# Two fused blocks on one core: new orders for all five engines, scores and attend scores in longer runs

## The chip, the cores and the metric

The kernel runs on one core of a Trainium2 chip. Its time is the device time of one execution in microseconds (us); of several runs the median counts. A core has five engines that work in parallel, each through its own list of instructions in order: TensorE (PE, matrix products into PSUM banks), VectorE (DVE), ScalarE (ACT), GpSimd (POOL) and SyncE (SP, which here issues the DMAs). They wait for one another by semaphores.

## The reference

Input are 8 batches of 256 tokens with 128 numbers each, in float32. Two blocks follow each other:

```
xn = layernorm(x)
x  = x + attention(xn; 16 query heads, 4 key heads, width 8) + experts(xn)
       # attention: softmax(q k^T / sqrt(8)) v, then Wo
       # experts: top 2 of 8 gates, but all experts share relu(xn w1) w2
xn = layernorm(x)
x  = x + ssm(xn) + ffn(xn)
       # ssm: xz = xn W_in; causal convolution of 4 taps; silu; dt = softplus(xs W_dt + b)
       #      h_t = h_(t-1) * exp(-A dt_t) + B_t, 16 states; y = sum(h) + D xs; (y silu(z)) W_out
       # ffn: silu(xn w1) * (xn w2), gelu(. h1), gelu(. h2), then w3; 512 wide
```

## The kernel before, in words

The program is written as pieces: a piece is a few instructions of one engine, with the waits that they need. `run_order` goes through a text with the names of the pieces, one text for each engine (`ORDERS`, lines 72 to 125), and issues them in that order, counting how often each name came. So the whole order of the work is that table. What an instruction waits for is written in the piece; nothing is planned at run time.

First block, one batch of 256 tokens after the other, on TensorE:

- `S` (`scores`): the scores of two heads for 128 queries, laid out queries by keys, 16 pieces a batch. VectorE takes the row maximum of each (`M`, line 680). The first 8 are one float32 product (line 388); from piece 8 on each is two bf16 products over 48 rows (line 399). There are three PSUM banks, so score n waits until maximum n-3 is done.
- `A` (`attend_scores`, line 422): the scores again, transposed and with the negated maximum folded in as three more rows, 16 a batch; ScalarE exponentiates each (`E`, line 630), from three other banks. For batches 0 to 6 they use rows 64 to 114 of the array, and the scores rows 0 to 47. For batch 7 they take 115 rows.
- `pv` (line 435): probabilities times values, 4 a batch; `o_out` on ScalarE copies the sum (line 565), `heads` (line 445) transposes it, `back` and `proj_out` bring it through Wo.
- `ffn_in` and `ffn_out` (lines 459, 467) are the experts, `v_gate`, `project` and `project_keys` the projections, `max_rows` (line 489) transposes the maxima, `xn_transposes` the input. `warm` (line 513) are 16 pieces of two products whose result isn't used.
- At the start the keys are copied into four wide tiles on ScalarE (`own_keys`, line 615), each of which two of the first 8 scores need.

Second block, four groups of 512 tokens: `x_transposes`, `x_in`, `wx`, `step_in` on TensorE feed the state space part; `ffn`, `second` (line 1016) and `third` (line 1028) are the feed forward part. For each of 16 states `b` (line 989) spreads one row over the partitions into a bank, ScalarE makes the decays (`D`, line 1217), VectorE runs the recurrence (`scan`, line 1312, two a state), GpSimd adds them up (`add`, line 1368, two a state; four states may be held). `y` (line 1376) multiplies by the gate, `out` (lines 1089, 1099) projects. `b` of state s waits for the scans of state s-2. `b_in` on ScalarE (lines 1175, 1176) and `split` on GpSimd (lines 1381 to 1385) prepare the rows of the next group.

Some pieces share one bank, `half0` or `half1`. The names in `X_AFTER`, `Q_AFTER`, `M_AFTER`, `T_AFTER` and so on (lines 140 to 155) say after which piece the bank is taken over: x is the transposed input, q the query projection, v the values and gates, m the maxima, t the output on its way back, p the projection.

Of the kernel before, what the change touches and what calls it, by code (L numbers as in the profile page):

```python
# [65 lines left out]
def settled(eng, sem, v):  # L66
# [6 lines left out]
    sync="""x_in head x_in constants0 ffn_weights 2*put 2*put_keys x_in put put_keys fetch 2*put_keys 2*put put_keys  # L73
        put fetch put stack 2*rows put rows put fetch stack 3*put 3*rows fetch loads put_keys 3*put put_keys stack put
        2*rows put_keys rows fetch stack 2*put 3*rows stack fetch loads 3*put fetch 3*rows put loads stack rows put
        rows put rows fetch stack 6*rows loads 3*b_rows out b_rows 7*out landed""",
    tensor="""9*warm xn_transposes 2*warm project project_keys ffn_in warm v_gate S xn_transposes S warm ffn_in
        xn_transposes S xn_transposes S project_keys project 6*S ffn_out 2*S xn_transposes 2*S project ffn_in 2*S
        xn_transposes ffn_in max_rows 3*S 2*warm v_gate warm 3*S ffn_out S xn_transposes S 2*A S xn_transposes S A S
        project_keys S A S 2*A S project S A S A ffn_in A S A max_rows A S A S v_gate ffn_in S A S A S ffn_out project  # L80
        A S A S A S pv A S A S pv A S A S A S 2*pv A 2*S project heads A S A S max_rows A S pv v_gate A S A S A S pv
        back A S A S A S pv proj_out pv S 3*A S heads S 2*A S A S back ffn_in proj_out A S A S ffn_in A S A S A S
        max_rows ffn_out v_gate A S A S A S pv A S A S 3*pv S 2*A S A S heads A S A S project ffn_in A S A S back
        ffn_in A S proj_out ffn_out max_rows A S A S A S project ffn_in A S A S A S v_gate ffn_in v_gate A S A S
        ffn_out A S A S A S 2*pv S A S A S 2*pv S 2*A S A S heads max_rows S A S A back ffn_in A S proj_out ffn_in A S
        A S A S ffn_out A S A 2*S 3*pv S A S A S pv A S v_gate heads 2*A S A S back ffn_in proj_out A S A S max_rows
        ffn_in A S 2*A S x_transposes A S A S ffn_out A S A S x_in A S A S pv A S A S pv A S A pv A S A pv A S 2*A S
        heads A ffn 3*A pv 2*A max_rows ffn x_in 2*pv x_in A ffn x_in wx pv A 2*step_in back x_transposes heads ffn b
        A proj_out x_in A x_in b A pv second A second A x_in second A x_in b A wx A step_in b A pv A second b back A
        second A b second A proj_out b A 2*pv 2*b second heads second b step_in third back b third b third proj_out b  # L90
        third b 3*third b third x_transposes b 2*x_in b 2*ffn x_in b x_in ffn wx ffn b 3*out b second 2*out b out
        second b second b second b 2*second b step_in b second b second step_in b third x_transposes b third b x_in b
        2*third x_in third b third b 2*third b ffn x_in ffn b x_in b wx ffn step_in out b ffn out b out b out second
        out b second out b second b 2*second b 2*second b second b step_in b 2*third 2*b 2*third b third b 2*third b
        third b 2*ffn out b ffn b out ffn 2*out 2*b 2*second b second b 2*second b second b second b second 2*out b
        2*third 2*b 6*third 6*out""",
    scalar="""roots deviation0 xn_out deviation0 wide_out q_out k_out own_keys normalised own_keys relu xn_out
# [1402 lines left out]
```

## Time and profile before

| | us |
|---|---|
| median of 3 runs | 357.62 (357.3 to 357.71) |
| the profiled execution | 357.89 |
| its span | 356.1 |
| TensorE busy by the records | 348.4 (98%) |
| VectorE busy | 307.3 (86%) |
| ScalarE busy | 291.1 (82%) |
| GpSimd busy | 232.6 (65%) |

A matmul record's end is modelled and overlaps the next, so the busy time of TensorE hides short waits. The distance from one matmul's start to the next one's start tells more. The profiled execution's own time is 1.8 us above its span.

### The profile page before, as it was taken

The page shows a single profiled execution, that of the slowest core. Times are in us where ns is not written, and L with a number is a line of the kernel's source. Part 1 is how long each engine was busy: PE and PEld are TensorE (multiplying, and loading weights), DVE is VectorE, ACT ScalarE, POOL GpSimd, SP SyncE. Part 2 cuts the span into 40 slices and gives each one's busy share as a digit, 9 for nine tenths or more (in the row PEclk, how much of TensorE's full clock was granted, in tenths as well). Part 3 has the DMA queues.
Part 4 walks back from the last instruction along what each step waited for, and adds up shares of the span by engine and source line. Part 5 has one row for each costly group of instructions (what it writes and reads, how often), then busy time and mean ns, then how long its engine had stood idle before and what let it go on. Part 6 is the DMA issues. An engine that isn't in the chain of part 4 may idle for free.

```text
span 356.1 us, 5750 instructions
## 1 busy us (share of the span) xinstructions
PE 348.4 (98%) x1754; PEld 181.6 (51%) x1754; DVE 307.3 (86%) x530; ACT 291.1 (82%) x508; POOL 232.6 (65%) x294
## 2 busy tenths in 40 slices
PE   7999999999999999999999999999999999999996
PEld 5556544747565523443444447444457444564446
DVE  5898889988899886499999999999999989799940
ACT  3875976877787885898899999999999999899620
POOL 0484457214420601344999989999898999999980
PEclk9999999999999999999999999999999999999999
DMA  4455776586724003000000000000000200000000
GB/s 167 130 146 119 146 204 143 81 131 196 197 78 74 6 0 123 22 1 2 0 0 23 3 0 24 15 0 1 1 2 0 67 0 1 2 0 1 31 0 29
DMA packets 28943, 19.26 MB, mean 54 GB/s; under 512 B 4241, under 2 KB 27889, under 8 KB 28657
## 3 DMA queue, kind: packets, MB, share of 16 engines
q1 hardware_dynamic: 28912, 18.90, 21.8%
q8 instruction: 14, 0.23, 0.3%
q14 instruction: 17, 0.13, 0.1%
HBM read 13.32 MB, written 5.37 MB: 53 GB/s over the span
## 4 chain that ended last, share of the span: by engine, by line
PE 87%; issue 5%; DVE 4%; POOL 2%; ACT 1%; POOLq 0%
PE bank L1028 15%; PE bank L1016 13%; PE bank L435 6%; PE bank L422 5%; PE bank L467 4%; PE bank L399 4%; PE bank L459 4%; PE bank L1005 4%; PE bank L1099 4%; PE bank L1006 4%; PE bank L989 4%; PE bank L1072 3%; PE bank L1052 3%; POOL acc L1368 2%; PE bank L388 2%
## 5 line engine op out<-in xcount | busy, mean ns | idle before, releaser
L1368 POOL TENSOR_TENSOR acc<-acc,hb 128x512 f32<-128x512 f32 x128 | 158.2, 1273 | 19.2 <-DVE hb L1312 18.9
L1312 DVE TENSOR_TENSOR_SCAN hb<-da,bank 128x512 f32<-128x512 f32 x128 | 146.0, 1200 | 9.2 <-PE bank L989 9.1
L680 DVE TENSOR_REDUCE mx<-bank 128x2 f32<-128x512 f32 x128 | 81.7, 682 | 7.2 <-PE bank L399 5.9
L1217 ACT ACTIVATE da<-dt,nega 128x510 f32<-128x510 f32 x128 | 81.4, 710 | 0.3 <-DVE da L1336 0.2
L1016 PE MATMUL bank<-sil,ld 128*128 128x512 f32 x128 | 59.5, 593 | 0.0
L1028 PE MATMUL bank<-gelu,ld 128*128 128x512 f32 x128 | 58.0, 592 | 0.0
L630 ACT ACTIVATE pt<-bank 128x512 f32<-128x512 f32 x72 | 39.6, 602 | 6.2 <-PE bank L422 4.5
L422 PE MATMUL bank<-q_st,k_st 51*128 51x512 bf16 (+1 forms) x128 | 39.8, 382 | 0.4
L1028 PEld LDWEIGHTS bank<-gelu,ld 128*128 128x128 f32 x128 | 24.3, 190 | 26.8 <-issue 25.4
L399 PE MATMUL bank<-k_st,q_st 48*128 48x256 bf16 x240 | 36.9, 272 | 0.0
L1016 PEld LDWEIGHTS bank<-sil,ld 128*128 128x128 f32 x128 | 24.0, 190 | 24.6 <-issue 22.9
L630 ACT ACTIVATE hb<-bank 128x512 f32<-128x512 f32 x56 | 30.4, 600 | 4.4 <-PE bank L422 4.4
L989 PE MATMUL bank<-b_parts,sel 96*128 96x512 bf16 x64 | 23.8, 382 | 0.5 <-DVE hb L1312 0.4
L399 PEld LDWEIGHTS bank<-k_st,q_st 48*128 48x128 bf16 x240 | 17.4, 94 | 10.6 <-DVE mx L680 5.9
L422 PEld LDWEIGHTS bank<-q_st,k_st 51*128 51x128 bf16 (+1 forms) x128 | 9.3, 94 | 22.7 <-ACT pt L630 11.0
L435 PE MATMUL bank<-pt,v_sb 128*32 128x512 f32 x144 | 18.6, 602 | 0.0
L1281 DVE SCALAR_TENSOR_TENSOR xc<-bank,ld,xc 128x510 f32<-128x510 f32 (+2 forms) x24 | 17.7, 742 | 0.7
L1099 PEld LDWEIGHTS bank<-ld,gelu 128*128 128x128 f32 x128 | 16.0, 192 | 3.4 <-issue 3.2
L1052 PE MATMUL bank<-xnT,ld 128*128 128x512 f32 x32 | 16.7, 607 | 0.9 <-ACT xnT L1168 0.9
L459 PE MATMUL bank<-xnT,w 128*128 128x256 f32 x64 | 17.1, 390 | 0.0
L1217 ACT ACT_TABLE_LOAD x13 | 16.7, 1283 | 0.2
L1005 PE MATMUL bank<-xnT,ld 128*128 128x512 f32 x32 | 16.7, 603 | 0.0
(166 smaller groups left out, 527.3 us busy)
## 6 DMA issues: line engine op xcount, KB each, us to landing
q_st<-q_scr SPq DMA_DIRECT2D x15, 192.0 KB, 3.8
q_st<-q_scr SPq DMA_DIRECT2D x7, 384.0 KB, 5.3
ld<-in_pack SPq DMA_DIRECT2D x2, 1024.0 KB, 5.5
q_scr<-qk_parts SPq DMA_DIRECT2D x8, 192.0 KB, 2.5
k_st<-k_scr SPq DMA_DIRECT2D x14, 96.0 KB, 4.5
q_scr<-qk_parts SPq DMA_DIRECT2D x8, 128.0 KB, 2.7
out<-x SPq DMA_DIRECT2D x8, 128.0 KB, 2.0
ld<-in_pack SPq DMA_DIRECT2D x1, 968.0 KB, 7.6
```

Of the source, the lines that this page charges most:

```text
L399: last = mm(score_bank(b, n)[:, j * T:(j + 1) * T], q_st[b % 2][0:ROWS, 2 * pair + j, q * P:(q + 1) * P], k_st[b % 2][0:ROWS, 2 * pair // ...
L422: mm(st(b, n)[:, :], k_st[b % 2][lo:, kv, kt * P:(kt + 1) * P], q_st[b % 2][lo:, h0:h0 + 2, :].rearrange("r h n -> r (h n)"), start=True, ...
L435: last = mm(bP[kv * VW:(kv + 1) * VW, :], v_sb[b % NV][:, kt, kv, at:at + VW], prob(b, 4 * grp + kv), start=(grp == 0), stop=(grp == 3))
L459: last = mm(bP[:, j * T:(j + 1) * T], w1[:, c * P:(c + 1) * P], xnT[b], start=True, stop=True)
L630: act(prob(b, n), st(b, n)[:, :], ACT.Exp, scale=HD ** -0.5).then_inc(p_ok, 1)
L680: eng.tensor_reduce(mx[:, 2 * pair:2 * pair + 2, q], score_bank(b, n)[:, :].rearrange("p (h k) -> p h k", h=2), AX.X, ALU.max).then_inc(mx ...
L989: mm(b_bank(g, s)[:, :], sel[:, s, :], b_parts[:, g % 2, :], start=True, stop=True).then_inc(b_ps, 1)
L1016: last = mm(f_bank(g, c)[:, :], h1[:, k, c * P:(c + 1) * P], sil[:, k, :], start=(k == 0), stop=(k == KC - 1))
L1028: last = mm(f_bank(g, c)[:, :], h2[:, k, c * P:(c + 1) * P], g2[:, k, :], start=(k == 0), stop=(k == KC - 1))
L1217: act(da(n)[:, :, 1:T], dt[:, g % 2, c, :].rearrange("p (b n) -> p b n", b=GB)[:, :, 1:T], ACT.Exp, scale=nega[:, c, s:s + 1]).then_inc(da ...
L1312: eng.tensor_tensor_scan(hb[:, s % NPAIR, c, :], da(n).rearrange("p b n -> p (b n)"), b_bank(g, s)[:, :], 0.0, ALU.mult, ALU.add).then_inc ...
L1368: TT(acc[:, g % 2, c, :], acc[:, g % 2, c, :], hb[:, s % NPAIR, c, :], ALU.add).then_inc(add_ok, 1)
```

## The change

All five texts of `ORDERS` are replaced by others with the same pieces, each as often as before. No piece is changed. Since pieces stand in another order, three of the tables that name after whom a shared bank is taken over are changed as well. The diff (the table cut to one line of each kind):

```diff
 ORDERS = dict(
-        2*warm xn_transposes 2*warm project project_keys ffn_in warm v_gate S xn_transposes S warm ffn_in
...
-        A S A S A S pv A S A S pv A S A S A S 2*pv A 2*S project heads A S A S max_rows A S pv v_gate A S A S A S pv
+        A S A S A S 2*pv A S A S A S pv A S A S A S pv A S max_rows heads A S A S A S v_gate pv A S A S A S back pv
...
-Q_AFTER = "x0 x3 x4 k2 v2 q4 v4 m4"
+Q_AFTER = "x0 x3 x4 k2 v2 p0 v4 m4"
...
-M_AFTER = "x5 q3 q5 p1 p2 v6 p4 m6"
-T_AFTER = "v3 p0 q6 m5 v7 m7 p5 p6"
+M_AFTER = "x5 q3 q4 p1 p2 v6 p4 m6"
+T_AFTER = "v3 q5 q6 m5 v7 m7 p5 p6"
```

**TensorE, batch 1, around `heads` of batch 0.** L422 is an attend score, L399 x2 a score, L445 `heads`, L489 `max_rows`, L435 `pv`. Before:

```order
L520 MATMUL bank<-xnT,head 128x256
L445 MATMUL bank<-head,o_sb 128x128 x4
L422 MATMUL bank<-q_st,k_st 128x512
L399 MATMUL bank<-k_st,q_st 128x256 x2
L422 MATMUL bank<-q_st,k_st 128x512
L399 MATMUL bank<-k_st,q_st 128x256 x2
L489 MATMUL bank<-head,mx 32x128
L422 MATMUL bank<-q_st,k_st 128x512
L399 MATMUL bank<-k_st,q_st 128x256 x2
L435 MATMUL bank<-pt,v_sb 32x512 x4
```

Now:

```order
L422 MATMUL bank<-q_st,k_st 128x512
L399 MATMUL bank<-k_st,q_st 128x256 x2
L489 MATMUL bank<-head,mx 32x128
L445 MATMUL bank<-head,o_sb 128x128 x4
L422 MATMUL bank<-q_st,k_st 128x512
L399 MATMUL bank<-k_st,q_st 128x256 x2
L422 MATMUL bank<-q_st,k_st 128x512
L399 MATMUL bank<-k_st,q_st 128x256 x2
L422 MATMUL bank<-q_st,k_st 128x512
L399 MATMUL bank<-k_st,q_st 128x256 x2
L497 MATMUL bank<-cst,xnT 128x40 x2
```

After `heads` stood a run of two pairs and a run of one, with `max_rows` between; now there is one run of three pairs, and `max_rows` stands before `heads`. Only one pair and `max_rows` are left between the last `pv` of batch 0 and `heads`; before these were an attend score, two scores and a `project`.

**ScalarE, the start.** L615 x2 is a piece of `own_keys`, L559 x2 a normalised batch, L569 a copy of transposed input, L582 a `relu`. Before:

```order
L604 ACTIVATE qk_parts<-bank,cst 32x256
L615 ACTIVATE hb<-dt,cst 128x256 x2
L559 ACTIVATE xn<-x_sb,nmr,rstd 128x128 x2
L615 ACTIVATE hb<-dt,cst 128x256 x2
L582 ACTIVATE hT<-bank 128x512
L569 ACTIVATE xnT<-bank 128x256
L559 ACTIVATE xn<-x_sb,nmr,rstd 128x128 x4
L569 ACTIVATE xnT<-bank 128x256 x2
```

Now:

```order
L604 ACTIVATE qk_parts<-bank,cst 32x256
L559 ACTIVATE xn<-x_sb,nmr,rstd 128x128 x2
L615 ACTIVATE hb<-dt,cst 128x256 x2
L559 ACTIVATE xn<-x_sb,nmr,rstd 128x128 x2
L569 ACTIVATE xnT<-bank 128x256
L559 ACTIVATE xn<-x_sb,nmr,rstd 128x128 x2
L569 ACTIVATE xnT<-bank 128x256
L582 ACTIVATE hT<-bank 128x512
L569 ACTIVATE xnT<-bank 128x256
```

The first `own_keys` comes behind a normalised batch, and the fourth (not in these rows) behind the query and key copies of the next group, right ahead of the first exponential of the gates.

**TensorE, the end.** L989 is a `b`, L1028 x2 a `third`, L1016 x2 a `second`, L1089 and L1099 are `out`. Before:

```order
L1099 MATMUL bank<-ld,gelu 128x128 x4
L989 MATMUL bank<-b_parts,sel 128x512
L1028 MATMUL bank<-gelu,ld 128x512 x4
L989 MATMUL bank<-b_parts,sel 128x512 x2
L1028 MATMUL bank<-gelu,ld 128x512 x12
L1089 MATMUL bank<-wout_half,y 128x128 x8
```

Now:

```order
L989 MATMUL bank<-b_parts,sel 128x512
L1028 MATMUL bank<-gelu,ld 128x512 x4
L989 MATMUL bank<-b_parts,sel 128x512
L1028 MATMUL bank<-gelu,ld 128x512 x4
L989 MATMUL bank<-b_parts,sel 128x512
L1028 MATMUL bank<-gelu,ld 128x512 x8
L1089 MATMUL bank<-wout_half,y 128x128 x8
```

The last `b` stood ahead of six pieces of `third`, now ahead of four.

## Rows read from the trace of the kernel before

**Rows 1.** The page: the chain of work that ended last, by engine.

```profile
PE 87%; issue 5%; DVE 4%; POOL 2%; ACT 1%; POOLq 0%
```

**Rows 2.** Busy time by stretch: us, then PE, PEld, DVE, ACT, POOL, PEclk, DMA share.

```profile
45.00:97.00 52.00, 51.68 (x432) 28.51 (x432) 45.79 (x109) 39.15 (x91) 21.47 (x56) 1.00 0.71 162
...
150.00:180.00 30.00, 29.07 (x122) 11.83 (x122) 27.79 (x39) 27.21 (x49) 17.94 (x15) 1.00 0.00 1
180.00:348.00 168.00, 167.44 (x568) 84.80 (x567) 153.16 (x166) 151.09 (x214) 159.59 (x139) 1.00 0.03 9
```

**Rows 3.** The chain in order of time: start, us, what.

```profile
12.70 0.86 PE bank L459 x4
...
66.63 1.06 PE bank L459 x4
...
217.89 0.22 PE bank L989
218.11 1.72 PE bank L1016 x4
...
261.62 0.57 PE bank L1061 x16
```

**Rows 4.** Timeline of PE: start, us, instruction; three pairs, then the maxima.

```profile
67.62 0.39 PE L422 MATMUL bank<-q_st,k_st 51*128 51x512 bf16 x1
...
67.85 0.38 PE L422 MATMUL bank<-q_st,k_st 51*128 51x512 bf16 x1
...
68.38 0.28 PE L489 MATMUL bank<-head,mx 128*32 128x128 f32 x1
```

**Rows 5.** Timeline of PE and of ACT around the first `heads`.

```profile
49.95 1.92 PE L435 MATMUL bank<-hb,v_sb 128*32 128x512 f32 x16
...
51.81 0.61 PE L399 MATMUL bank<-k_st,q_st 48*128 48x256 bf16 x4
52.35 0.70 PE L520 MATMUL bank<-xnT,head 128*128 128x256 f32 x2
...
51.94 0.60 ACT L565 ACTIVATE o_sb<-bank 128x512 f32<-128x512 f32 x1 [0.77 <-PE bank L435]
```

**Rows 6.** Timeline of ACT and PE, the start.

```profile
9.27 0.89 ACT L615 ACTIVATE hb<-dt,cst 128x256 f32<-128x256 f32 x2
...
10.30 1.10 PE L388 MATMUL bank<-hb,dt 128*128 128x512 f32 x2
...
20.43 0.61 PE L399 MATMUL bank<-k_st,q_st 48*128 48x256 bf16 x4
```

**Rows 7.** Timeline of PE and ACT, the rows of group 1.

```profile
164.16 0.65 PE L1061 MATMUL bank<-xs,wx_p 128*32 128x128 f32 x16
164.92 0.39 PE L422 MATMUL bank<-q_st,k_st 115*128 115x512 bf16 x1
165.37 1.98 PE L1072 MATMUL bank<-xs,ld 128*128 128x512 f32 x4
...
165.05 0.27 ACT L1176 ACTIVATE b_full<-bank 128x128 f32<-128x128 f32 x1
```

**Rows 8.** Timeline of PE, DVE and POOL, the end.

```profile
337.43 4.55 DVE L1312 TENSOR_TENSOR_SCAN hb<-da,bank 128x512 f32<-128x512 f32 x4 [0.71 <-PE bank L989]
...
347.74 1.95 PE L1089 MATMUL bank<-wout_half,y 128*128 128x128 f32 x16
...
343.61 2.49 POOL L1376 TENSOR_TENSOR y<-acc,zs 128x512 f32<-128x512 f32 x2
```

**Rows 9.** Timeline of DVE: row maxima behind two runs of three pairs.

```profile
56.70 1.89 DVE L680 TENSOR_REDUCE mx<-bank 128x2 f32<-128x512 f32 x3
```

**Rows 10.** Timeline of PE: those two runs, first row of each.

```profile
56.24 0.39 PE L422 MATMUL bank<-q_st,k_st 51*128 51x512 bf16 x1
...
58.37 0.39 PE L422 MATMUL bank<-q_st,k_st 51*128 51x512 bf16 x1
```

**Rows 11.** The waits: engine, line, waited for, us in total, times, longest.

```profile
DVE mx L680 <- PE bank L399: 5.9, 12, 1.5
```

More of the change, by code:

```diff
@@ L72 @@
 ORDERS = dict(
[L73 to L80, printed above, removed]
-        A S A S A S pv A S A S pv A S A S A S 2*pv A 2*S project heads A S A S max_rows A S pv v_gate A S A S A S pv
[L82 to L96, printed above, removed]
@@ L121 @@
-    gpsimd="""biased G ones split_k split_q 3*G shifted0 4*G biased split_q maxima_split 8*G split_q maxima_split 8*G
-        split_q split_k maxima_split G biased G split_q 5*G maxima_split 5*G split_q 4*G maxima_split 10*G split_q 3*G
-        maxima_split 7*G maxima_split 4*G constants maxima_split split 2*start 8*add start 6*add start 7*add split
-        4*add shifted 7*add 2*y 2*start add split 30*add y add y 3*add 2*start 9*add split 23*add 2*y 29*add 2*y""",
+    sync="""x_in head x_in constants0 ffn_weights x_in put 3*put_keys 2*put fetch put 3*put_keys 2*put fetch put stack
+        put 2*rows put rows stack fetch put 2*rows put rows put put_keys loads fetch 2*put stack put loads 3*rows
+        2*put_keys fetch stack rows put rows 2*put rows fetch 3*put stack loads 3*rows put fetch stack 3*rows put
+        loads put fetch stack 6*rows 3*b_rows 4*out b_rows 4*out landed""",
@@ new lines @@
+    scalar="""roots deviation0 xn_out deviation0 wide_out q_out k_out normalised own_keys normalised xn_out normalised
+        xn_out relu xn_out own_keys k_out own_keys q_out deviation0 own_keys gate_exp relu 2*normalised xn_out q_out
+        normalised relu xn_out normalised negated_maxima relu gate_exp xn_out E xn_out E k_out 3*E q_out 4*E
+        negated_maxima relu 3*E gate_exp relu 3*E q_out 8*E o_out 2*E negated_maxima 4*E gate_exp 3*E o_out 3*E q_out
+        2*E relu 3*E relu negated_maxima 5*E gate_exp 3*E o_out 2*E q_out 2*E relu 3*E relu E negated_maxima 2*E q_out
+        E relu 2*E gate_exp relu 3*E gate_exp 6*E o_out 2*E negated_maxima 2*E relu E relu 3*E deviation 5*E o_out 3*E
+        gate_exp 2*E relu 3*E negated_maxima relu E x_out 2*E decay_rates 5*E taps 3*E o_out 4*E negated_maxima E sil
+        2*E gate_x 3*E sil taps gate_z E gate_x b_in E gate_z o_out E sil 2*dt sil E x_out 2*D E taps 2*D E 2*D taps
+        gate_x D gate_z E 3*D gate_x D E D E D E D gate_z D b_in E 2*D E D E 2*D E D E D E D 2*gelu o_out 2*gelu 2*dt
+        12*D deviation hid normalise hid x_out 2*hid 2*taps sil gate_x sil gate_x 2*gate_z normalise 2*sil b_in 29*D
+        4*gelu dt x_out dt D taps 5*D taps 3*D 4*hid sil gate_x gate_z gate_x sil gate_z 3*D 2*sil b_in 17*D gelu dt D
+        3*gelu dt 13*D 4*hid 2*sil 3*D 2*sil 12*D 2*gelu 3*D 2*gelu 3*D 4*hid""",
@@ L125 @@
+    gpsimd="""G biased ones split_k split_q 2*G shifted0 5*G split_q maxima_split 8*G biased split_k split_q
+        maxima_split 8*G biased split_q maxima_split 5*G split_q 3*G maxima_split 5*G split_q 3*G maxima_split split_q
+        12*G maxima_split 7*G maxima_split 5*G constants maxima_split split 2*start 7*add split 5*add start 5*add
+        start 9*add shifted 5*add y add y 2*start 2*add split 31*add 2*y 3*add start 4*add split 10*add start 18*add y
+        add y 27*add 2*y""",
 )
```

52 lines of the change are left out of this document (29 added, 23 removed).

## The prediction, made before the changed kernel ran

> **What bounds the kernel now.** I read the page first: the chain that ended last is TensorE for 87%, and no other engine has more than 4% of it [rows 1]. Then the busy time by stretch. From 45 to 97 us TensorE is busy for 51.68 of 52 us, VectorE for 45.79 and ScalarE for 39.15; from 180 to 348 us TensorE for 167.44 of 168, GpSimd for 159.59 [rows 2]. As the busy time of TensorE hides waits, I looked at the starts. In the chain a feed forward half takes 1.72 us for 4 records, again and again, with a `b` of 0.22 between [rows 3], and in a run of three pairs the first two attend scores start at 67.62 and 67.85: 0.22 us from pair to pair, whatever VectorE and ScalarE do [rows 4]. So TensorE works like a conveyor, from some 16 us to the last `out`, with short waits at a handful of places. As it has the same pieces before and after, the time changes by two things alone: what it costs TensorE to go from one kind of piece to another, and its waits.
>
> **What a border costs.** Four records of `ffn_in` take 0.86 us where a full-size product stands on either side, and 1.06 where a run of scores does [rows 3]: 0.20 for two borders, so about 0.1 for each. A run of three pairs shows the same: three steps of 0.22 are 0.66, and from its first row to the `max_rows` behind it are 0.76 [rows 4]. Between a score run and `pv` or `max_rows`, and between those and full-size products, the starts show the same 0.09 to 0.10. A border here is a change among three shapes: products over part of the rows (bf16 scores and attend scores of batches 0 to 6), products into 32 columns (`pv`, `max_rows`, `project_keys`, `wx`), and full ones. Between two full ones none is seen: `b`, over 96 rows, costs 0.22 and the `second` behind it 1.72 for its four records [rows 3].
>
> **What a step costs.** An attend score lies beside a score: both together take 0.22 us [rows 4]. One alone takes the same 0.22: a run of one attend score and two scores goes from 51.81 to 52.35, that is two steps and a border, 0.54 [rows 5].
>
> **The change, part by part.**
>
> *Score runs, TensorE.* I counted in both orders. There are 57 runs of partial-row products before and 53 after; 10 of them were three full pairs, now 18. The changes of shape go from 144 to 136. Eight borders less, at 0.095: -0.76 us. The steps of all runs together go from 137 to 135, since fewer scores and attend scores stand without a partner: two steps less at 0.218, -0.44. Together -1.2 us, directly on the conveyor.
>
> *The start.* ScalarE now normalises a batch ahead of the first `own_keys`. That batch takes 0.8 us (as long as a piece of `own_keys`, 9.27 to 10.16), so the first wide keys are done at 10.9 instead of 10.16, and the first score, at 10.30 before, can start at 10.9 [rows 6]. The `xn_transposes` in front of it takes 0.22 of that. Further on `ffn_in` 1 meets a later `relu`, some 0.4, and the fourth `own_keys` ends about 0.8 later. Against that the key copies come 1 us earlier. Walking these through with the rows' durations, the first bf16 score starts at about 20.85 instead of 20.43 [rows 6]; 0.22 of this is a `warm` that stood behind it. I take +0.2. The ends: -0.3, if the earlier third normalisation group (its shift comes sooner from GpSimd) shortens a wait, and +0.8, the whole of the later keys.
>
> *`heads`.* The last `pv` of batch 0 ends at 51.87 (49.95 and 1.92), the copy `o_sb` runs from 51.94 to 52.54, and `heads` needs it, so it could not start before 52.6. Before, the run of 0.54 and a `project` of 0.53, from 51.81 on, cover that [rows 5]. Now one pair (0.22), a border and `max_rows` (0.12) are there and end at 52.25: TensorE waits about 0.4. For batches 1 and 3 runs of 0.76 and some 0.7 stand there; the cover falls short by 0.1 each. Sum +0.6; the ends are 0, if ScalarE's copy comes out of its queue at once and something else was late anyway, and +1.2, twice my value.
>
> *`wx` and `step_in` of group 1.* `step_in` stood one attend score behind `wx`, and waited for the copy of `wx` on ScalarE, 165.05 to 165.32; it started at 165.37 where 165.14 would do, and the `wx` before it took 0.76 to the next start, where that of group 3 takes 0.57 [rows 7]. Now a `second`, a `b` and two attend scores (2.4 us) lie between. -0.4. On ScalarE that copy comes about 4 us of work later; `step_in` comes 4.8 later too, so that it doesn't matter. GpSimd has its `split` of group 1 far earlier, after 7 adds rather than 21, and may wait there for the copy. Between 150 and 180 us it is busy for 17.94 of 30 us [rows 2], so there is room.
>
> *The end.* The last `b` stands 4 records x 4 = 16 records ahead of `out` in place of 24. At 0.43 each it would start at 347.74 - 6.9 - 0.2 = 340.7. Its two scans, 2.3 us, and the last add and the two `y` behind (1.2 and 2.5) end at about 347.2. `out` starts at 347.74, so it is still covered, but with 0.5 us in place of 1.6 [rows 8]. 0, at most +0.5.
>
> *The rest.* Other moves in the second block (sync's order, table loads of ScalarE: 38 before and 37 after, decays up to 8 us of ScalarE's work later) lie beside the conveyor. ScalarE works 151.09 of 168 us there [rows 2], and each late decay that I followed still comes ahead of its scan. 0; if one is late by 1 us, one scan waits for it, which costs nothing as long as `b` and the adds have a state in hand.
>
> Sum: -1.2 + 0.2 + 0.6 - 0.4 = -0.8 us. The profiled execution took 357.89 us, which is 0.27 above the median 357.62; against the median the forecast is 356.8 us. Its own range, by the ends above and by what the waits that exist can do, is 355.6 to 357.6.
>
> **Rivals.**
>
> *The banks hold the longer runs back (slower).* A score waits for the maximum three before it. VectorE takes 1.89 us for three of them [rows 9], TensorE makes three in 0.66. Of two runs of three that start 2.13 us apart, the third score of the second, two pairs behind its start, came at 58.8, and the maximum that it needs ended at 58.59 [rows 9, 10]: 0.23 to spare. A run, one `pv` and a run, as the new order has in batch 1 and later, start 0.76 + 0.96 = 1.72 apart: 0.18 too early. This decides if VectorE can't win back in the gaps: it is busy for 45.79 of 52 us already [rows 2]. For the eight additional runs of three at 0.4 each it is 3.2, so the time is 357.6 - 0.8 + 3.2 = 360.0; at 0.25 each it is 358.8, which I take as its value. Against it: in the old order eight of the ten runs of three take 0.76, without a wait, as in [rows 4]; the other two 0.78 and 0.82. The Trainium skill says in TensorEngine Tiling (Array Packing), section PSUM Bottleneck, that tiling speeds up TensorE but not the emptying of PSUM, which may become the bottleneck; that is this rival. The trace agrees with it only at places: by it alone a pair could not go faster than a maximum, 0.63, and three pairs go in 0.66.
>
> *VectorE takes back what TensorE gains (no change).* VectorE is busy for 88% of the attention stretch [rows 2]. If its list runs through at some place without a gap, what comes before may be 1 us earlier and what comes behind isn't: 357.6. For it: VectorE's work is the same to the last piece. Against it: in the whole kernel its maxima waited 5.9 us for scores [rows 11].
>
> *Old waits go too (faster still).* With the rates above, TensorE's pieces and borders add up to 347 us. Of the span of 356.1, some 4.5 us lie ahead of the first product and behind the last; 4 to 5 us are waits. A new order may have half: 357.6 - 0.8 - 2.2 = 354.6.
>
> *The last states come too late (no change).* If the end above misses by 1 us: 357.6.
>
> **How the numbers follow.** Forecast case 0.45 (356.8), banks 0.22 (358.8), VectorE takes back 0.15 (357.6), old waits go 0.13 (354.6), late end 0.05 (357.6). A measurement of this kernel can tell 0.2%, 0.7 us, from no change. Of the forecast case 0.6 lies below 356.9, the rest within; the bank case lies above 358.3 for nine parts in ten. So faster is 0.27 + 0.13 and a little of the others, which I round to 0.45; slower is 0.20 plus 0.05 of the late end and the start's upper end, 0.25; the same 0.30. The range takes in old waits and banks at their values: 354.4 to 359.2.
>
> **What would show it.** Right: runs of three pairs at 0.76, 53 runs, the chain still TensorE, the first `heads` about 0.45 late, `out` of the last group starting right behind the last `third`. Wrong: runs of three at 0.9 or more, with weight loads of L399 waiting for L680, would be the banks; if the runs are clean and `step_in` of group 1 (before at 165.37 [rows 7]) comes no earlier than its place in the order asks, 4.8 us later, at 170.2, VectorE took it back. A first bf16 score after 21.3 us would mean that the start was underrated.

## The result, and the profile after

| | before | after |
|---|---|---|
| median, us | 357.78 (357.3 to 358.02, 10 runs) | 360.12 (359.11 to 364.17, 10 runs) |
| ratio | | 1.0081, 95% interval 1.0062 to 1.01 |
| the profiled execution | 357.89 | 364.17 |
| its span | 356.1 | 362.4 |

The kernel got 0.8% slower; 356.8 was forecast, and the range ended at 359.2. Eight of the ten runs lie between 359.11 and 360.32; the profiled one is 4 us above the median and another (362.61) 2.5. Over the whole time the granted TensorE clock was 0.991 in the profiled one and 0.995 in the other, and 0.999 or 1.00 in the eight. So two things have to be explained: an ordinary loss, and one that some executions have.

The chain of waits by engine of the kernel after reads as before, with VectorE at 7% for 4 [rows 1]:

```profile
PE 88%; DVE 7%; issue 2%; ACT 2%; POOL 0%; DVEq 0%; ACTq 0%; POOLq 0%
```

Busy time by stretch of the kernel after (us, then PE, PEld, DVE, ACT, POOL, PEclk, DMA share and GB/s), to be held against [rows 2]: in the attention stretch TensorE is busy for 49.23 of 52 us where it was 51.68, and in the last row it is as busy as before (167.71 us for 167.44).

```profile
45.00:97.00 52.00, 49.23 (x402) 28.71 (x405) 44.43 (x109) 35.70 (x79) 20.32 (x57) 0.98 0.74 164
150.00:180.00 30.00, 28.73 (x116) 11.99 (x115) 25.03 (x34) 27.92 (x49) 15.05 (x17) 1.00 0.04 11
180.00:348.00 168.00, 167.71 (x582) 84.05 (x582) 158.06 (x175) 154.20 (x221) 161.13 (x138) 1.00 0.03 8
```

**The long wait of the profiled execution.** Timeline of TensorE, batch 4:

```profile
91.97 0.54 PE L497 MATMUL bank<-cst,xnT 128*128 128x40 f32 x4
94.86 0.58 PE L422 MATMUL bank<-q_st,k_st 51*128 51x512 bf16 x1 [2.35 <-issue]
...
95.24 0.63 PE L422 MATMUL bank<-q_st,k_st 51*128 51x512 bf16 x1
...
96.25 3.64 PE L435 MATMUL bank<-pt,v_sb 128*32 128x512 f32 x16
```

The first attend score of batch 4 waits 2.35 us, and behind it pairs come every 0.4 us instead of 0.22 [rows 4], and 16 `pv` records take 3.64 us. By stretch:

```profile
85.00:90.00 5.00, 5.00 (x37) 3.27 (x35) 3.72 (x12) 3.81 (x10) 3.10 (x8) 1.00 1.06 272
90.00:95.00 5.00, 2.65 (x25) 2.47 (x24) 2.97 (x11) 1.71 (x5) 1.87 (x10) 0.94 1.20 170
95.00:100.00 5.00, 5.00 (x29) 1.61 (x29) 1.89 (x3) 1.57 (x3) 0.00 (x0) 0.50 0.16 33
100.00:105.00 5.00, 4.94 (x40) 1.52 (x33) 2.76 (x5) 3.15 (x7) 0.00 (x0) 0.87 0.00 0
```

The granted clock falls to 0.50, the lower of the two levels (1.2 GHz), near the end of the wait, stays there over the next slice and is 0.87 in the one after. The slices from 90 to 105 us lack 0.06, 0.50 and 0.13 of full clock, each times 5 us: some 3.4 us beside the wait itself (an estimate). What the attend score waits for are three rows of 8 KB that SyncE copies into its tile. SyncE's timeline (start and length of the issue):

```profile
83.22 0.45 SPq L358 DMA_DIRECT2D ld<-in_pack  x1
84.22 2.39 SPq L340 DMA_DIRECT2D q_st<-m_parts  x3
```

The new order puts `loads` 2, weights of the second block, ahead of `rows` 12 to 14. The issues with their size and the time to landing (of three: the median), from the same trace:

```profile
ld<-in_pack SPq DMA_DIRECT2D x1, 1024.0 KB, 10.6
...
q_st<-m_parts SPq DMA_DIRECT2D x3, 8.0 KB, 6.0
```

The last of the three was issued at 85.75 and landed at 94.77, 0.09 us ahead of the attend score. Before, the load was issued at 89.72, behind the rows, and these took a median of 1.9 us (3.8 for the first).

**What the prediction had named.** TensorE of the kernel after: a run of three pairs [rows 4], `heads` of batch 0 [rows 5], the start [rows 6], `wx` and `step_in` of group 1 [rows 7], the end [rows 8].

```profile
68.39 0.39 PE L422 MATMUL bank<-q_st,k_st 51*128 51x512 bf16 x1
...
69.15 0.28 PE L489 MATMUL bank<-head,mx 128*32 128x128 f32 x1
...
53.85 0.28 PE L489 MATMUL bank<-head,mx 128*32 128x128 f32 x1
54.25 0.63 PE L445 MATMUL bank<-head,o_sb 128*128 128x128 f32 x4
...
21.01 0.61 PE L399 MATMUL bank<-k_st,q_st 48*128 48x256 bf16 x4
...
174.22 0.64 PE L1061 MATMUL bank<-xs,wx_p 128*32 128x128 f32 x16 [0.57 <-issue]
...
177.46 1.88 PE L1072 MATMUL bank<-xs,ld 128*128 128x512 f32 x4
...
354.05 1.95 PE L1089 MATMUL bank<-wout_half,y 128*128 128x128 f32 x16
```

This run of three pairs takes 0.76, as before; the others follow with the experiments. `heads` comes 0.40 behind `max_rows`, 0.28 more than its 0.12. The last `y` on GpSimd, below, ends at 353.61, 0.44 ahead of `out`:

```profile
351.12 2.49 POOL L1376 TENSOR_TENSOR y<-acc,zs 128x512 f32<-128x512 f32 x2
```

### The profile page after: what moved, and what is told of

The parts are those of the page before. It is cut to its first block, busy times and chain, and to the rows that moved or that the text cites. A ratio compares the mean times of both kernels' runs of the same rounds, so it can differ in the third digit from the quotient of the medians.

```text
span 362.4 us, 5749 instructions
## 1 busy us (share of the span) xinstructions
PE 350.8 (97%) x1754; PEld 180.9 (50%) x1754; DVE 308.8 (85%) x530; ACT 289.7 (80%) x507; POOL 233.2 (64%) x294
## 4 chain that ended last, share of the span: by engine, by line
PE 88%; DVE 7%; issue 2%; ACT 2%; POOL 0%; DVEq 0%; ACTq 0%; POOLq 0%
PE bank L1028 15%; PE bank L1016 14%; PE bank L435 8%; PE bank L422 5%; DVE mx L680 4%; PE bank L1052 4%; PE bank L1099 4%; PE bank L989 4%; PE bank L1005 4%; PE bank L1072 4%; PE bank L1006 4%; PE bank L467 4%; PE bank L459 3%; PE bank L399 3%; PE bank L1089 2%
## 5 line engine op out<-in xcount | busy, mean ns | idle before, releaser
L680 DVE TENSOR_REDUCE mx<-bank 128x2 f32<-128x512 f32 x128 | 81.7, 681 | 13.4 <-PE bank L399 11.2
L1016 PE MATMUL bank<-sil,ld 128*128 128x512 f32 x128 | 58.9, 592 | 0.0
L1028 PE MATMUL bank<-gelu,ld 128*128 128x512 f32 x128 | 58.4, 592 | 0.0
L422 PE MATMUL bank<-q_st,k_st 51*128 51x512 bf16 (+1 forms) x128 | 39.5, 387 | 2.4 <-issue 2.4
L1028 PEld LDWEIGHTS bank<-gelu,ld 128*128 128x128 f32 x128 | 24.1, 190 | 26.6 <-issue 26.1
L399 PE MATMUL bank<-k_st,q_st 48*128 48x256 bf16 x240 | 37.2, 275 | 0.2 <-DVE mx L680 0.2
L1016 PEld LDWEIGHTS bank<-sil,ld 128*128 128x128 f32 x128 | 23.8, 190 | 23.9 <-issue 23.3
L989 PE MATMUL bank<-b_parts,sel 96*128 96x512 bf16 x64 | 24.1, 382 | 0.5 <-DVE hb L1312 0.3
L422 PEld LDWEIGHTS bank<-q_st,k_st 51*128 51x128 bf16 (+1 forms) x128 | 9.3, 94 | 29.6 <-ACT pt L630 12.1
L399 PEld LDWEIGHTS bank<-k_st,q_st 48*128 48x128 bf16 x240 | 17.5, 95 | 7.9 <-DVE mx L680 3.6
L845 POOL TENSOR_TENSOR m_parts<-negm,m_parts 32x128 bf16<-32x128 f32 x8 | 3.3, 418 | 26.1 <-ACT negm L576 26.0
L435 PE MATMUL bank<-pt,v_sb 128*32 128x512 f32 x144 | 19.9, 652 | 0.0
L1205 ACT ACTIVATE gelu<-bank,ld 128x512 f32<-128x512 f32 x14 | 9.1, 686 | 11.8 <-PE bank L1028 11.7
L1099 PEld LDWEIGHTS bank<-ld,gelu 128*128 128x128 f32 x128 | 16.4, 192 | 3.0 <-issue 2.6
L822 POOL TENSOR_TENSOR gd<-srt 128x16 f32<-128x16 f32 x8 | 1.7, 214 | 24.4 <-issue 13.9
```

The source lines that it names most:

```text
L399: last = mm(score_bank(b, n)[:, j * T:(j + 1) * T], q_st[b % 2][0:ROWS, 2 * pair + j, q * P:(q + 1) * P], k_st[b % 2][0:ROWS, 2 * pair // ...
L422: mm(st(b, n)[:, :], k_st[b % 2][lo:, kv, kt * P:(kt + 1) * P], q_st[b % 2][lo:, h0:h0 + 2, :].rearrange("r h n -> r (h n)"), start=True, ...
L435: last = mm(bP[kv * VW:(kv + 1) * VW, :], v_sb[b % NV][:, kt, kv, at:at + VW], prob(b, 4 * grp + kv), start=(grp == 0), stop=(grp == 3))
L680: eng.tensor_reduce(mx[:, 2 * pair:2 * pair + 2, q], score_bank(b, n)[:, :].rearrange("p (h k) -> p h k", h=2), AX.X, ALU.max).then_inc(mx ...
L989: mm(b_bank(g, s)[:, :], sel[:, s, :], b_parts[:, g % 2, :], start=True, stop=True).then_inc(b_ps, 1)
L1016: last = mm(f_bank(g, c)[:, :], h1[:, k, c * P:(c + 1) * P], sil[:, k, :], start=(k == 0), stop=(k == KC - 1))
```

## The experiments

Each was timed in five rounds, beside runs of the kernel before on the same chip. "Trace" is the profiled span less before's 356.1, both rounded to 0.1.

| kernel | us, median | ratio to before, 95% interval | trace |
|---|---|---|---|
| e1, after again | 359.10 (358.55 to 361.09) | 1.0042, 1.0026 to 1.0058 | +0.7 |
| e2, load 2 later | 359.11 | 1.0034, 1.0022 to 1.0046 | +1.2 |
| e3, all loads later | 359.11 | 1.0033, 1.002 to 1.0045 | +1.2 |
| e4, before, load 2 early | 364.06 | 1.0177, 1.0156 to 1.0198 | +5.3 |
| e5, old start | 358.52 | 1.0023, 1.001 to 1.0035 | +0.9 |
| e6, old to batch 2 | 361.37 | 1.0101, 1.0077 to 1.0125 | +4.3 |
| e7, old first block | 359.04 | 1.0041, 1.0029 to 1.0053 | +1.1 |
| e8, before, 18 borders more | 361.29 | 1.0104, 1.0092 to 1.0117 | +3.4 |
| e9, old to 51 us | 357.87 | 1.0004, 0.9996 to 1.0013 | 0.0 |
| e10, new from 51 to 130 us | 360.96 | 1.0102, 1.0085 to 1.0119 | +2.4 |
| e11, e10, taps later | 360.51 | 1.0086, 1.0073 to 1.0098 | +2.9 |
| e12, before, one batch first | 358.39 | 1.0024, 1.0014 to 1.0034 | +0.7 |
| e13, e11, seam complete | 357.55 | 0.9994, 0.9985 to 1.0003 | -0.4 |
| e14, e3, own keys first | 358.74 | 1.0035, 1.0022 to 1.0047 | +0.8 |

**e1 to e4: the load ahead of the rows.** e1 is the kernel after, unchanged. e2 moves load 2 behind the rows:

```diff
-    ... 2*put rows fetch 3*put stack loads 3*rows put fetch stack 3*rows put loads ...
+    ... 2*put rows fetch 3*put stack 3*rows put loads fetch stack 3*rows put loads ...
```

e3 moves all four loads so (0 behind fetch 3, 1 behind fetch 5, 2 as in e2, 3 behind the last rows). e4 does the opposite to the kernel before:

```diff
-    ... 3*put fetch 3*rows put loads stack rows put ...
+    ... 3*put fetch loads 3*rows put stack rows put ...
```

> The changed kernel once more, to see the profile of another execution: the profiled one took 4 us more than the median of its kind, with a wait of 2.35 us ahead of the first attend score of batch 4 and the granted clock at 0.5 from 95 to 100 us. Theory DMA (the weight load `loads` 2 is queued ahead of the rows of maxima `rows` 12 to 14, whose last part landed at 94.77): the same wait is there, 1 to 3 us long, the third part of the maxima lands 5 us or more after its issue, the median is again 360.1, and an execution of about 360 has less or nothing of the clock's dip. Rival banks (longer runs wait for the maxima and the exponentials): no wait for a DMA at batch 4 in an ordinary execution; 2.3 us more than before are spread over the runs of three pairs, which take 0.8 to 0.9 instead of 0.76.

> The changed kernel with one DMA moved on SyncE's list: `loads` 2 (1 MB of weights) stands behind `put` 21, so behind `rows` 12 to 14, in place of ahead of them. Theory DMA: the rows of batch 4 land within 2 to 3 us, the first attend score of batch 4 waits for nothing, the clock stays at 1.0, and the time falls by 2 to 3.5 us, to 356.8 to 358. Rival banks: no change within 0.5 us, 360.1.

> The changed kernel with all four weight loads at the places that they had on SyncE's list before the change (behind `fetch` 3, `fetch` 5, `put` 21 and `rows` 23). Theory DMA: at or below the kernel with `loads` 2 alone moved, by 0 to 1 us, as the others stand ahead of the maxima of batch 2 and of the query parts of batch 7 too. Rival banks: 360.1, no change.

> The kernel before the change with `loads` 2 moved ahead of `rows` 12 to 14 and behind `fetch` 6, all else as it was. Theory DMA: slower than before by 1 to 3 us, with a wait of the first attend score of batch 4 for the maxima. Rival (the load's place doesn't matter, the runs do): within 0.5 us of 357.7.

e1 had its median at 359.10, not at the expected 360.1. That is the same kernel as in the result, 1.6 us above the kernel before where it was 2.3; where the rest of the 2.3 comes from is open, since there is no trace of an ordinary execution of that series. e2 and e3 have the median of e1, and not the 357 to 358 that the theory gave them; only the upper end moved, from 361.09 to 359.41 and 359.18. In e1's profile the three rows took a median of 5.6 us to land and the attend score didn't wait. So moving the load takes nothing off the 1.6 us. That it costs the new order some executions is argued: the result's profile shows it for one, and the other slow one of that series has the lower clock too; e1's 361.09 has it not (1.00), so something else made it, and twelve executions of e2 and e3 are few. In the old order the same move costs 6.5 us in the median (364.06 against 357.54) and 5.7 at least, where 1 to 3 were expected. e4's chain in order of time, and its stretches:

```profile
91.61 3.62 issue
95.23 0.37 PE bank L423
```

```profile
90.00:95.00 5.00, 1.61 (x15) 1.42 (x13) 2.01 (x6) 2.40 (x11) 0.78 (x4) 1.00 0.79 202
95.00:100.00 5.00, 4.77 (x31) 1.69 (x32) 2.18 (x7) 1.68 (x4) 1.07 (x4) 0.66 0.03 8
```

The same wait, 3.62 us (the old order has `v_gate` elsewhere, so there is less in front of the attend score), and the same fall of the clock behind it. Of the four executions two had a mean clock of 0.995 (363.24 and 363.42 us) and two 0.991 (364.69 and 365.04).

**e5, e12, e14: the start.** e5 is e3 with the old orders of all engines up to the first attend score. e12 is the kernel before with one move on ScalarE, e14 is e3 with that move taken back:

```diff
 e12, ScalarE
-    ... q_out k_out own_keys normalised own_keys relu ...
+    ... q_out k_out normalised 2*own_keys relu ...
 e14, ScalarE
-    ... q_out k_out normalised own_keys normalised xn_out ...
+    ... q_out k_out own_keys 2*normalised xn_out ...
```

> The changed kernel with its four loads behind the rows (as in e3), and with the old orders of all five engines up to the first attend score (24 scores on TensorE, up to the first exponential on ScalarE). Theory: the start was underrated. In the trace of e3 the first bf16 score comes 1.03 us later than before, and nothing behind gives that back, so this kernel is 1.0 us below e3's 359.1: 358.1. Rival: the late start is taken up by a wait behind it (VectorE's list, the next normalised group), and the time stays at 359.1.

> The kernel before, with one move on ScalarE alone: the first normalised batch (0.77 us) stands ahead of the first own_keys, as in the new order. Theory (the start term): the first wide keys and the first scores come about 0.7 us later, and 0.3 to 0.7 of it reaches the end: 358.1. Rival (TensorE has other work there, as the prediction had it, or a later wait takes it up): 357.6.

> The changed kernel with its loads behind the rows (e3) and one move back on ScalarE: the first own_keys ahead of the first normalised batch. Theory (e12 backwards): 0.6 to 0.8 us off e3's 359.1, so 358.4. Rival (what e5 showed: a late start is partly taken up by later waits, here 24 to 51 us): 358.8. Rival (TensorE's own order there has other work between): 359.1.

e12 cost 0.9 us (358.39 against 357.46 beside it). Its TensorE:

```profile
10.97 1.10 PE L389 MATMUL bank<-hb,dt 128*128 128x512 f32 x2 [0.67 <-ACT hb L616]
...
21.10 0.61 PE L400 MATMUL bank<-k_st,q_st 48*128 48x256 bf16 x4
```

(Its lines are one further: L389 is L388.) The first score waits 0.67 us for the keys, the first bf16 score comes 0.67 late [rows 6], and at the end of the trace 0.77 are left: in the old order there is no cover.

In the new order it is another matter. TensorE of e3 and, behind the dots, of e14, ahead of the first score:

```profile
11.39 0.41 PE L506 MATMUL bank<-head,xn 128*128 128x128 f32 x2 [0.66 <-DVE srt L711]
...
11.00 0.41 PE L506 MATMUL bank<-head,xn 128*128 128x128 f32 x2 [0.66 <-ACT xn L559]
```

The new order has `xn_transposes` of batch 1 ahead of the first score and right behind `v_gate`, and by `X_AFTER` it may write only when VectorE has read what `v_gate` left (`v_out`, line 711). That ends at 11.24 in e3 and 10.86 in e14, 0.15 and 0.14 ahead of the transposes, so TensorE waits 0.66 in both, whatever the order of the keys (in e14 the normalised batch that it also needs ends at about the same moment, and the profile names that). In e3 the first keys are done at 11.25, and the first score, right behind the transposes, starts at 11.64. The two kernels are then the same: counted from the first `project`, the first bf16 score comes after 14.16 us in both, and the end after 350.0 in both, as in e1. What differs is the head ahead of the first `project`, 6.91 us in e14 and 7.30 in e3. So e14 gave nothing that its move could claim: its ratio to before is 1.0035 where e3 has 1.0033, and the 0.37 us between their medians, taken on two chips, don't show in the ratios.

e5 has 0.59 less than e3 in the medians, but its trace doesn't gain either: the first bf16 score is back at 20.32, 13.45 behind the first `project`, and by attend score 16 it is 1.06 behind the kernel before again; the end comes 350.1 behind the first `project`. Its head is shorter (6.87). The five traces with the new order's ten `warm` ahead of the first `xn_transposes` start it at 5.82 to 6.10, the eleven with nine at 5.53 to 5.67; that may be where e5's 0.59 lies, but no run changes this alone. So the theory of these three holds in the old order, and the rival ("a late start is taken up by later waits") in the new one.

**e6, e9, e10, e11, e13: which stretch.** These kernels follow the old orders on all five engines up to some moment and the new ones behind it, or old, new, old; loads behind the rows in all. As an example the texts of TensorE at e9's cut:

```diff
 kernel before:
     ... A S A S A S pv | A 2*S project heads A S A S max_rows ...
 e9, the new order behind the cut:
     ... A S A S A S pv | A S A S pv A S max_rows heads A S A S A S ...
```

> As e5, but the old orders reach to score 64 and attend score 41 (the first two and a half batches). Theory: the new attention order gains in borders there what it loses in waits, e3 lies +1.1 to +1.4 us behind at attend scores 32 and 48, so 357.8, some 0.3 below e5. Rival (the new attention order is itself faster and only the start is bad): 358.5 or more, since this takes its gain away.

> The changed kernel with its loads behind the rows, and the old orders of all engines up to the same moment, some 51 us (TensorE up to pv 2, ScalarE up to the first o_out, VectorE up to maximum 44, the row and key transfers that are issued by then). Theory: of e3's distance to before 1.3 us arises ahead of 51 us (TensorE comes to pv 3 1.29 us late, with an order that asks for 0.15 less), and what lies behind gains and loses about the same: 359.1 - 1.3 = 357.8. Rival (as in e5, the waits come back behind the cut, because the new order wants its pieces at other times): 358.5. Rival (the wait of e6 came from any seam between two orders, not from transfers that were out of step with ScalarE): 360 or more, with a slow TensorE behind a long wait.

> As e9, and from attend score 106 on (some 130 us) the old orders again: only the attention between 51 and 130 us is new. Theory: there the new order has 1.1 us less of borders and steps and costs some 0.6 of waits, so it gains 0.4 on before: 357.5 - 0.4 = 357.1, and less than e9. Rival (the borders are hidden or not worth their price there): 357.5 or more. Rival (the seam at 130 us doesn't fit and costs a wait as in e7): 358.5.

e9 fits the theory: 357.87 for 357.8. In the balance all the ordinary loss is made in the first 51 us. e6, expected at 357.8, lost 3.5 us more than e9, since its cut was not at the same moment on all engines: ScalarE kept the old order up to its 40th exponential (some 71 us), SyncE only for 39 pieces (some 45 us). ScalarE and TensorE of e6:

```profile
54.40 0.47 ACT L593 ACTIVATE qk<-bank,cst 128x256 f32<-128x256 f32 x1 [2.17 <-DMA q_scr<-qk_parts]
```

```profile
55.38 0.27 PE L489 MATMUL bank<-head,mx 128*32 128x128 f32 x1 [2.16 <-ACT qk_parts L594]
...
57.17 1.08 PE L497 MATMUL bank<-cst,xnT 128*128 128x40 f32 x4
```

```profile
48.00:56.00 8.00, 5.84 (x55) 2.54 (x54) 4.84 (x11) 5.03 (x11) 3.30 (x6) 1.00 0.60 162
56.00:64.00 8.00, 8.00 (x48) 3.09 (x48) 5.17 (x12) 3.94 (x11) 6.29 (x13) 0.57 0.36 97
64.00:72.00 8.00, 7.85 (x62) 4.18 (x56) 7.27 (x17) 5.32 (x11) 0.53 (x4) 1.00 0.52 72
```

A transfer out of step stops ScalarE for 2.17 us, that stops TensorE for 2.16, and the clock is 0.57 for the eight us behind it. The trace is 4.3 us longer than before's. Three of the six executions had a lower mean clock (0.990 to 0.995) and took 362.2 to 362.8; the other three (1.00) took 359.8 to 360.5. So the clock makes some 2 us of it.

e10, e11 and e13 were to isolate the new attention between 51 and 130 us. e10 and e11, expected at 357.1 and 357.2, failed at the second cut, each time by a wait that belongs to neither order:

```diff
 e10, VectorE (old text behind maximum 124)
     ... M | other_taps 3*M heads clear_keys x_mul ffn_mul ...
 e11, VectorE
+    ... M | 3*M heads other_taps clear_keys x_mul ffn_mul ...
 e13, VectorE and ScalarE
+    ... M | 3*M heads other_taps ffn_mul x_mul clear_keys ...
-    ... E | gate_x E sil 4*E negated_maxima ...
+    ... E | E sil 3*E gate_x E negated_maxima ...
```

> As e10, with the other taps of the first convolution (2.3 us on VectorE) behind the last maxima and heads 5, where the new order has them; in e10 they stood ahead of three maxima and two scores waited 2.2 us. Theory: e10's loss is that seam alone, so this is 3.4 us below e10, 357.2: old up to 51 us, new up to 130 us, old again, with the gain of the new middle, 0.3 to 0.4 on before. Rival (the new middle gains nothing): 357.6 or more.

> As e11, with the rest of the seam mended: on ScalarE the first gate_x, which needs the convolution, behind four more exponentials, and on VectorE the feed forward product ahead of it. In e11 that gate_x waited 2.74 us for VectorE, the exponentials stood behind it, and TensorE came 1.7 and 1.1 us late. Theory: without those waits this is 2.9 + 0.3 below e11's 360.5: 357.2, the new middle's gain. Rival (there is always a next wait at this seam, as conv and the products come 2 to 3 us later than in the old order): 358.0 or more. Rival (the new middle gains nothing): 357.5.

TensorE of e10 (a score waits for VectorE, which runs 2.3 us of taps), and ScalarE of e11 (`gate_x` waits for the taps, the exponentials stand behind it):

```profile
131.66 0.39 PE L399 MATMUL bank<-k_st,q_st 48*128 48x256 bf16 x2 [1.99 <-DVE mx L680]
```

```profile
133.03 0.63 ACT L1152 ACTIVATE xs<-xc 128x512 f32<-128x512 f32 x1 [2.74 <-DVE xc L1281]
```

e10's profiled execution is the only one of its six with the clock at 1.00; the others had 0.995 or 0.991. Of e11's five, four had 0.995, and the one at 1.00 took 359.83. With both waits gone e13 is 3.0 us below e11, with the clock at 1.00 or 0.999 in all executions. At 357.55 beside 357.61 it can't be told from the kernel before; its trace is 0.36 shorter than before's. It is the best of these versions, and not shown to beat the kernel before.

The starts of the profiled executions say where a difference arises. The kernels have the same set of pieces ahead of these places of TensorE's list (the first row is the first `project`, a landmark only):

| TensorE has done | before | e1 | e3 | e9 | e13 | borders fewer in the new order |
|---|---|---|---|---|---|---|
| the head, up to `project` 0 | 6.95 | 6.76 | 7.30 | 6.95 | 6.96 | |
| all ahead of the first bf16 score | 20.43 | 20.92 | 21.46 | 20.52 | 20.40 | 0 |
| its first 64 pieces | 34.48 | 34.30 | 34.84 | 34.32 | 34.22 | 2 |
| its first 117 pieces | 50.83 | 51.58 | 52.12 | 50.79 | 50.70 | 3 |
| its first 349 | 129.52 | 129.85 | 130.39 | 129.18 | 129.10 | 8 |
| its first 422 | 183.65 | 184.42 | 184.97 | 183.75 | 183.28 | 8 |
| all (span) | 356.06 | 356.75 | 357.31 | 356.08 | 355.70 | 8 |

e1 and e3 differ by 0.5 us from the head on: so much does the head of one execution differ from another's, and behind it the two are the same. e3's execution took 359.1, the median, so I go by it. Of its 1.25 us the head has 0.35. At the first bf16 score another 0.68 are lost, but after 64 pieces nothing of that is left (27.54 us behind `project` 0, where before had 27.53): the late start is taken up. Between pieces 64 and 117, from 34 to 51 us, 0.93 are lost again, in e1 as in e3. From 117 to 349 e3 gained 0.42, where five borders less ask for 0.48 and the steps for something more: the rest went into new waits. From 349 to 422, the passage to the second block, it lost 0.45. Behind that the distance stays.

The largest wait between pieces 64 and 117 is that of `project` 3, which by the new `Q_AFTER`, as by the old, may write only behind ScalarE's copy of the keys (line 604). Before and, behind the dots, e3:

```profile
37.24 0.67 PE L520 MATMUL bank<-xnT,head 128*128 128x256 f32 x2 [0.23 <-ACT qk_parts L604]
...
37.73 0.67 PE L520 MATMUL bank<-xnT,head 128*128 128x256 f32 x2 [0.51 <-ACT qk_parts L604]
```

In both it starts 1.76 to 1.77 us behind `project_keys` (35.48 and 35.96), but six pieces stood between them before and three now. In e5 the wait is 0.58, and `project` 3 starts 30.4 us behind `project` 0 in both e3 and e5: here the gain of an early start is gone. Smaller ones follow in e3, 0.15 of `max_rows` for the maxima and 0.25 of `ffn_out` for a `relu`. No run takes them away by themselves.

**The longer runs.** Of the 18 runs of three full pairs in e1 and e3, eleven take 0.76 to 0.80 us to the start of the piece behind, seven 0.82 to 1.08. In three of the seven the third score waits for a maximum; of these the longest, from 51.90 to 52.83 in e3, shows it in the weight loads:

```profile
52.51 0.11 PEld L399 LDWEIGHTS bank<-k_st,q_st 48*128 48x128 bf16 x2 [0.27 <-DVE mx L680]
```

The three take 0.93, 0.89 and 0.88, together 0.42 above 0.76. So the banks do hold some longer runs back, by little. The three longest, 1.04, 1.04 and 1.08, are waits of the `back` and the `ffn_out` behind the run.

**e7: the second block alone.** Old orders up to the last attend score, new ones behind.

On TensorE at the cut:

```diff
-    ... 2*pv b | b second heads second b step_in third back ...
+    ... 2*pv b | b 2*second heads b step_in back third ...
```

> The old orders up to the last attend score; only the second block (from the eighth b on) is in the new order, the loads behind the rows. Theory: all of the difference arises in the first block and at its seam; e3's second block runs at a constant distance to before, so 357.5 to 357.6, no change to before (357.54 measured beside it). Rival (the second block's fewer waits are worth something and only the first block hides it): 357.0 or less. Rival (the new end costs, as its last b stands late): 358.0.

It came out 1.5 us above the theory. Up to its cut the trace is 0.4 ahead of before; then, on VectorE and on TensorE:

```profile
183.20 0.36 DVE L685 RECIPROCAL rden<-bank 128x32 f32<-128x32 f32 x1 [1.49 <-PE bank L445]
```

```profile
188.60 0.39 PE L989 MATMUL bank<-b_parts,sel 96*128 96x512 bf16 x1 [1.34 <-DVE hb L1312]
```

VectorE's old list has the work on `heads` 7 one scan early for the new TensorE list, which does a `second` more ahead of it; VectorE waits, its scans come late, and `b` waits for them. Again the seam, not the block: e7 says nothing on the new second block, and e3's constant distance says that it is worth next to nothing either way.

**e8: the price of a border.** The kernel before, with an attend score and a score moved between two full pieces at nine places:

```diff
-    ... ffn_in S A S A S ffn_out project A S A S A S pv ...
+    ... ffn_in S A S A S ffn_out A S project A S A S pv ...
```

> The kernel before, with one attend score and score moved between two full pieces at nine places of the attention stretch: 18 changes of shape more, same pieces, same count of steps. By the price of the prediction (0.095 us each) 18 cost 1.7 us, so 357.5 + 1.7 = 359.2. Rival: the price is seen only where nothing else waits, and the pairs now stand further apart, which gives VectorE room: 358.2 or less. Rival: the gap in the starts isn't caused by the change of shape at all: 357.5.

It cost 3.7 us (361.29 against 357.58), twice the forecast. TensorE at the place of the diff (`ffn_out`, the moved pair, `project`, two pairs, `pv`; the lines are one further than before's):

```profile
43.65 2.05 PE L468 MATMUL bank<-w,hT 128*128 128x128 f32 x16
45.64 0.39 PE L423 MATMUL bank<-q_st,k_st 51*128 51x512 bf16 x1
...
45.96 0.70 PE L521 MATMUL bank<-xnT,head 128*128 128x256 f32 x2
46.59 0.39 PE L423 MATMUL bank<-q_st,k_st 51*128 51x512 bf16 x1
...
47.13 1.07 PE L436 MATMUL bank<-pt,v_sb 128*32 128x512 f32 x8
```

In the kernel before these pieces start at 43.46 (`ffn_out`), 45.35 (`project`), 45.88 (three pairs) and 46.63 (`pv`). `ffn_out` takes 1.99 to the next start where it took 1.89: 0.10. The moved pair takes 0.32, 0.22 and 0.10. `project` takes 0.63 where it took 0.53: 0.10. The two pairs take 0.54 for 0.75, one step less. Together 3.48 for 3.17, so 0.31 for two more borders. A run between full pieces thus costs 0.3 beside its steps: 0.1 on the piece ahead, 0.1 on its own last start, and 0.1 on the piece behind. That is 0.15 a border, and nine such places make 2.7 us. At eight of the nine the piece behind the moved pair is 0.39 to 0.43 later, as here (0.42). At the ninth, ahead of `ffn_in` 8, it is 0.83, a wait on top. The rest, some 0.5, I haven't placed. The rivals with a border at less, or at nothing, are out.

## Why the prediction was wrong

The sum was -0.8; measured were +2.3 us in the result and +1.6 beside e1. Two steps failed: that new waits were priced at a few places only (the start, `heads`, `wx`, the end), and that SyncE's order was set to nothing.

*What bounds the kernel, the borders and the steps (-1.2).* The conveyor is right: in e9 and e13 the new attention passes from piece 117 to 349 faster than the old one. Two things are wrong. The price of a border was 0.15, not 0.095: the rows were right, but I counted the 0.20 that `ffn_in` shows and the 0.1 at the end of a run [rows 3, 4] as two readings of one price, where they add up to 0.3 for two borders. With it eight borders would be -1.2, and the sum -1.6. The steps are good to 0.2 us only: paired off neighbour by neighbour they are 133 and 132, one fewer, and not 137 and 135. And only 0.4 arrives from piece 117 to 349, where five borders ask for 0.48, by the new price 0.75; the rest went into waits, 0.42 of it into those of the longer runs for maxima.

*The waits that had no term.* This is the first step that failed, and most of the ordinary loss. Between pieces 64 and 117, in the attention of batch 0, the sum had nothing but a border's gain, and e1 and e3 lose 0.93 us there. The largest wait is `project` 3 behind `project_keys`, the case that the prediction had worked out for `heads`: the new order leaves fewer pieces between two that depend on each other through ScalarE. e9, with the old order up to piece 117, is at 357.87 against 357.59: the place is shown. The single waits are read from traces and not shown one by one.

*The start (+0.2, end +0.8).* The wait that ended last was another. The prediction had the later keys, 0.77 us of ScalarE, partly covered by TensorE's other work, 0.22 of it by the `xn_transposes` in front. It is that piece that waits, 0.66 us, for VectorE, and with the keys first (e14) it waits as long. The sign that it named, a first bf16 score after 21.3, was at 21.01 in the kernel after and 20.92 and 21.46 in e1 and e3, and says little: behind the first `project` the three have the same 14.16 us, where before had 13.48. By piece 64 it is taken up, and e5, without it, ends no earlier behind `project` 0. Only in the old order does such a delay last (e12: 0.67 there, 0.77 at the end, 0.9 in the timed runs). The head ahead of `project` 0 is 0.35 longer in e3 and 0.19 shorter in e1; the prediction had 0.22 for the `warm` that was moved forward.

*`heads` (+0.6).* In kind right: 0.28 for the first.

*`wx` and `step_in` (-0.4).* Half right. `wx` to the next start is 0.58, as forecast, but 0.57 stand in front of it, since `wx` takes a bank that VectorE's second product into `zs` (line 1258) has to empty: that ends at 169.06 in e3, and `wx` starts at 169.17. `step_in` starts at 172.41 in e3. Moved by the final distance of 1.25 that is 171.16, where its place in the order asks for 170.2 with no gain: 1 us late. By the table e3 loses 0.45 on this passage, so the term is some +0.5 rather than -0.4 (an estimate).

*The end (0).* Right: 0.44 of cover in place of the forecast 0.5.

*The rest (0: "sync's order ... lie beside the conveyor").* This is the second step that failed. I looked at the order of SyncE's list by its names and not at what a load of 1 MB does to transfers of 8 KB behind it, of which the next attend score needs the last. e4 prices it at 6.5 us in the old order. In the new one it is often just covered (in e1 the last row landed at 91.9, the attend score started at 92.35). It explains the profiled execution (364.17) and probably the 362.61, which had the lower clock too, not the median of e1: e2 and e3 have the same.

*The rivals.* The banks: true in kind, with 0.42 us over three runs in place of 2.0, and one run met the sign of 0.9 or more. That the rival's 358.8 lies near e1's 359.10 is luck. The waits of maxima for scores rose in the kernel after because TensorE stood still (11.2 us in all, the longest 4.5, against [rows 11]); in e1 and e3 they are 5.7. "VectorE takes back": true in part, in that each gain finds a wait behind it. "Slower" came mainly by waits that no rival named and by the one term that was set to nothing.

What stays open: why the loss was 2.3 us in the result and 1.6 beside e1, how the 0.93 divide between the waits from 34 to 51 us, how much of the head is the tenth `warm`, and the 361.09 of e1.

## What to carry to other kernels

Sum a new order over every queue, SyncE's too: for each large transfer ask which small ones stand behind it and who needs the last of them. Wherever one piece needs another by way of a second engine, count what stands between them before and after, at all such pairs and not only at the one that looks worst. A delay at the start went through to the end in one order (e12) and was taken up by a later wait in the other (e3, e5), so its price is read at the next wait that both share, not at the first late piece; and traces are best laid over each other at a landmark behind the head. And two orders that each run well can't be joined at will: a cut has to lie at the same moment on all engines, and four of the seven joined kernels (e6, e7, e10, e11) lost 1.5 us or more at the seam.

## What the runs showed of the hardware

- A load of 1 MB took 10.6 us; three transfers of 8 KB issued 1.0 to 2.5 us behind it landed after up to 9.0 us (median 6.0), where they took a median of 1.9 without it, and 2.5 in e2. The same in e4: 9.1 for the load, a median of 6.1 for the rows; and in e1 5.6 for the rows.
- Waits of TensorE of 2.35, 3.62, 2.16 and 1.57 us came with a granted clock of 0.50 (95 to 100 us, kernel after), 0.66 (95 to 100 us, e4), 0.57 (56 to 64 us, e6) and 0.66 (135 to 140 us, e11). Executions of one kernel differ in it: in e6 three of six kept a mean of 1.00 and took 359.8 to 360.5 us in place of 362.2 to 362.8, and in e10, with a wait of 1.99, one of six kept it. The kernel after, with the wait and the low clock, has a span 5.6 us longer than e1's (362.4 and 356.8) for a wait of 2.35, so the clock may double the price of a wait. Waits of 0.67 us (e12) and 0.51 (e3) left it at 1.00.
- A run of products over part of the rows between full ones costs 0.3 us beside its own steps: 0.1 each on the start behind the full piece ahead, on the end of the run, and on the full piece behind (e8).
